# Layer 0's expert block: scalings and sums in parts between transfers, and a 512-column fill after each transfer in place of a wait for an expert tile

## What is computed

```python
h = _layernorm(x) * (1 + cb) + sb                      # per batch element: scale, then shift
logits = einsum('bnc,ec->bne', h, router_w);  w, idx = top_k(softmax(logits), 2);  w /= w.sum(-1)
hid = gelu(einsum('bnc,efc->bnef', h, w1) + b1)        # 512 hidden columns
out_all = einsum('bnef,ecf->bnec', hid, w2) + b2
x = x + gb * sum_k(out_all[idx_k] * w_k)               # only the two chosen experts are computed
h = _layernorm(x) * (1 + ca1) + sa1                    # layer 1 begins
```

## Time and profile before

| what | value |
|---|---|
| median of three executions | 1414.41 us (1411.29 to 1415.12) |
| the profiled execution, its own time | 1412.28 us |
| its span in the trace | 1410.6 us |
| PE, DVE, ACT, POOL busy over the span | 90%, 73%, 65%, 36% |
| `experts0`, from the first load of rows to the next stage's first matmul | 185.88 to 403.18 us |
| in that stretch, mean granted clock of TensorE | 0.94 |

### The profile page before, as it was taken

The page is one execution under the profiler, slowest core; times in us unless marked ns, Lnnn a source line. Parts: engine busy times, 40 slices in busy tenths (PEclk is TensorE's granted clock), DMA queues, the critical chain, the costliest instruction groups (busy, mean ns, idle before and its releaser), DMA issues. The chain is left out here.

```text
span 1410.6 us, 28627 instructions
## 1 busy us (share of the span) xinstructions
PE 1275.9 (90%) x9145; PEld 817.9 (58%) x9146; DVE 1030.0 (73%) x2720; ACT 918.1 (65%) x1320; POOL 511.8 (36%) x608
## 2 busy tenths in 40 slices
PE   6999768989886778999999999998999989998999
PEld 3877668988863423333334433333434357778898
DVE  5656266667568669888888878888988857787554
ACT  4565523333355487888888878888888848774232
POOL 5337835466449242222201222220122200388800
PEclk9999779999988799999999999999999989999999
DMA  8980112332316722222222222222022014011211
GB/s 258 222 53 24 36 58 87 97 80 72 85 53 232 201 46 37 43 41 39 32 34 33 41 39 41 42 35 38 24 42 37 9 48 139 17 57 57 71 35 32
DMA packets 112673, 93.96 MB, mean 67 GB/s; under 512 B 20034, under 2 KB 98336, under 8 KB 112544
## 3 DMA queue, kind: packets, MB, share of 16 engines
q1 hardware_dynamic: 101192, 76.18, 25.0%
q0 software_dynamic: 6144, 12.73, 3.1%
q10 hardware_dynamic: 5208, 3.43, 1.0%
HBM read 50.40 MB, written 41.89 MB: 65 GB/s over the span
## 5 line engine op out<-in xcount | busy, mean ns | idle before, releaser
L2446 ACT ACTIVATE probs<-scores_ps 128x1024 f32<-128x1024 f32 x512 | 507.2, 1027 | 86.2 <-PE scores_ps L2473 81.5
L2473 PE MATMUL scores_ps<-q_pack,k_pack 64*128 64x512 f32 x1024 | 246.6, 494 | 36.1 <-ACT probs L2446 21.2
L2490 PE MATMUL pv_ps<-probs,v_pad 128*32 128x512 f32 x2048 | 275.9, 611 | 0.0
L2473 PEld LDWEIGHTS scores_ps<-q_pack,k_pack 64*128 64x128 f32 x1024 | 96.2, 185 | 309.6 <-issue 153.5
L2366 POOL TENSOR_TENSOR squares<-sparse_scores 128x512 f32<-128x512 f32 x32 | 41.0, 1280 | 474.2 <-DVE sparse_scores L2611 474.1
L1406 ACT ACTIVATE hidden_experts<-pre_experts 128x512 f32<-128x512 f32 x94 | 59.3, 631 | 130.2 <-DVE pre_experts L1340 66.5
L2683 DVE TENSOR_SCALAR_CACHE_REDUCE junk<-sparse_scores,at 128x1024 f32<-128x1024 f32 x96 | 122.8, 1279 | 3.4
L1428 PE MATMUL up_ps_experts<-x_t_experts,up_weights_now_experts 128*128 128x128 f32 x752 | 108.2, 289 | 16.4 <-issue 7.7
L1428 PEld LDWEIGHTS up_ps_experts<-x_t_experts,up_weights_now_experts 128*128 128x128 f32 x752 | 96.1, 200 | 22.6 <-DVE up_weights_now_experts L1335 11.1
L1435 PE MATMUL down_ps_experts<-weights_t,hidden_experts 128*128 x736 | 100.5, 281 | 0.2 <-issue 0.2
L1435 PEld LDWEIGHTS down_ps_experts<-weights_t,hidden_experts 128*128 128x128 f32 x736 | 92.7, 198 | 0.0
(11 more groups left out here) (416 smaller groups left out, 2493.0 us busy)
## 6 DMA issues: line engine op xcount, KB each, us to landing
q_pack<-q_pieces_dram SPq DMA_DIRECT2D x120, 64.0 KB
k_pack<-k_pieces_dram SPq DMA_DIRECT2D x120, 64.0 KB
expert_rows_dram<-zeros SPq DMA_DIRECT2D x1, 6400.0 KB, 23.0
x_rows_experts<-expert_rows_dram SPq DMA_DIRECT2D x25, 256.0 KB
expert_rows_dram<-y_rows_experts SPq DMA_DIRECT2D x46, 128.0 KB
q_pieces_dram<-q_pieces_prep SPq DMA_DIRECT2D x8, 512.0 KB, 3.6
k_pieces_dram<-k_pieces_prep SPq DMA_DIRECT2D x8, 512.0 KB, 4.1
expert_rows_dram<-zeros SPq DMA_DIRECT2D x1, 2640.0 KB, 40.0
```

The costliest lines, as they stand in the source:

```text
L2446: act.activation(probs[:, kt % 2, 2 * pair : 2 * pair + 2, c * 512 : c * 512 + 512], scores_ps[n % 2][:].rearrange("p (h t) -> p h t", h=2 ...
L2473: ins = pe.matmul(scores_ps[n % 2][:, head * 512 : head * 512 + 512], k_pack[group % 2][rows, pair, kt * P : kt * P + P].bitcast(F32R), q_ ...
L2490: ins = pe.matmul(pv_ps[32 * j : 32 * j + 32, c, :], v_pad[:, group % 2, kt, j, :], probs[:, kt % 2, j, c * 512 : c * 512 + 512], start=(k ...
```

## The change

The block in `front` and `experts0` is changed in four ways.

1. The scaling and shifting of b = 2 goes into `front`, behind its last send, as eight POOL instructions of 256 columns (`hq.2.0` to `hq.2.7`: four that multiply, then four that add). That of b = 3 is cut likewise, and one of its eight parts stands behind each of the first eight sends of b = 2.
2. The waits for tiles (`next_tile`) are gone. Behind each send and fetch in `experts0` POOL fills a tile that nothing reads (`unread`, 128 x 512), and waits for that fill.
3. The sums of b = 0 and 1 are cut in two halves, ten instructions of 512 columns each. Those of b = 0 stand behind fetches 1 to 10 of b = 1, in place of the fills. Of b = 1's, eight run in one go when its rows have landed, and two behind the first two fetches of b = 2. The fetches of b = 1 get a semaphore of their own.
4. DVE takes the statistics of b = 0 at step 16 in place of 13; both inversions on POOL stand behind the last fetch.

```diff
+QUARTERS = 4
+    def scale_and_shift_part(self, pool, step, b, i):
+        at = b * NT + i % QUARTERS * (NT // QUARTERS)
+        h = self.h[:, at : at + NT // QUARTERS, :]
+        if i == QUARTERS:
+            step.settle()
+        op, by = ((ALU.mult, CB), (ALU.add, SB))[i // QUARTERS]
+        step(pool.tensor_tensor(h, h, bc(self.mod0[:, b, MOD0_PARTS.index(by), :], NT // QUARTERS), op))
...
-sd.1.12 sd.1.13 sd.1.14 sd.1.15 wk.10 ce2.3.1 no2.3.1 tu2.3.1 h2t.3.1 lg.3.1 lgk.3.1 be.1 po.1 exps gates ix.1 te.1
+sd.1.12 sd.1.13 sd.1.14 sd.1.15 hq.2.0 hq.2.1 hq.2.2 hq.2.3 hq.2.4 hq.2.5 hq.2.6 hq.2.7 wk.10 ce2.3.1 no2.3.1 tu2.3.1 h2t.3.1 lg.3.1 lgk.3.1 be.1 po.1 exps gates ix.1 te.1
...
-    STATS_AT = (13, 20)
+    STATS_AT = (16, 20)
+    ADDED_FIRST = 8
...
-                tile_at = [0]
-                def next_tile():
-                    tile_at[0] += 1
-                    pool.wait_ge(y_ready, tile_at[0] + 2)
+                fills = [0]
+                def fill():
+                    fills[0] += 1
+                    pool.memset(unread[:], 0.0).then_inc(filled, 1)
+                    pool.wait_ge(filled, fills[0])
                 for b in range(B):
                     if b >= SENT_EARLY:
-                        moe.scale_and_shift(pool, step, b)
                         step.settle()
-                        moe.send_rows(g, pool, b, apart=next_tile)
+                        for i in range(SEND_PARTS):
+                            moe.send_rows(g, pool, b, i, SEND_PARTS, apart=fill)
+                            if b + 1 < B and i < 2 * QUARTERS:
+                                moe.scale_and_shift_part(pool, step, b + 1, i)
                     pool.wait_ge(g.rows_sent[b], 16 * 2 * NT)
                     pool.sem_inc(rows_here, moe.tiles)
                 pool.sem_inc(rows_here, max(moe.tiles, 2 * UNROLL))
-                for b in range(B - 1):
-                    pool.wait_ge(y_free, b * (2 * AHEAD) + (2 * AHEAD + 1))
-                    tile_at[0] = max(tile_at[0], (b + 1) * moe.tiles)
-                    gather(pool, g, picked, b, [(k, n) for k in range(2) for n in range(NT)], g.rows_picked, apart=next_tile)
-                    if 1 <= b <= EARLY:
-                        pool.wait_ge(var_ready, b)
-                        g.ln1.invert(pool, b - 1).then_inc(rstd_ready, 1)
-                    pool.wait_ge(g.rows_picked, (b + 1) * (16 * 2 * NT))
-                    if b < EARLY:
-                        for part in weighted_sum(g, picked, b, NT):
-                            part(pool, step)
+                sums = [weighted_sum(g, picked, b, NT // 2) for b in range(EARLY)]
+                def add_up(b):
+                    sums[b].pop(0)(pool, step)
+                    if not sums[b]:
                         pool.sem_inc(summed, 1)
+                def fetch(b, sem, of, behind):
+                    for i, (n, k) in enumerate([(n, k) for k in range(2) for n in range(NT)]):
+                        gather(pool, g, picked, b, [(k, n)], sem)
+                        if i not in behind:
+                            fill()
+                        else:
+                            if of == 0 and i == behind[0]:
+                                pool.wait_ge(g.rows_picked, 16 * 2 * NT)
+                            add_up(of)
+                pool.wait_ge(y_free, 2 * AHEAD + 1)
+                fetch(0, g.rows_picked, None, ())
+                pool.wait_ge(y_free, 2 * (2 * AHEAD) + 1)
+                fetch(1, g.second_picked, 0, range(1, 11))
+                pool.wait_ge(g.second_picked, 16 * 2 * NT)
+                for _ in range(ADDED_FIRST):
+                    add_up(1)
+                pool.wait_ge(y_free, 3 * (2 * AHEAD) + 1)
+                fetch(2, g.rows_picked, 1, range(10 - ADDED_FIRST))
+                for b in range(EARLY):
+                    pool.wait_ge(var_ready, b + 1)
+                    g.ln1.invert(pool, b).then_inc(rstd_ready, 1)
+                pool.wait_ge(g.rows_picked, 2 * (16 * 2 * NT))
                 pool.wait_ge(rstd_ready, EARLY)
```

More of the change, by code:

```diff
@@ L615, in scale_and_shift, with scale_and_shift_part @@
                     moe.scale_and_shift(pool, step, b)
+                def scale_and_shift_part(b, i):
+                    if i == 0:
+                        for h in range(2):
+                            wait_made(pool, "tu2", b, h)
+                    moe.scale_and_shift_part(pool, step, b, i)
                 def send(b, q):
@@ L635, in _ @@
                         h2=scale_and_shift,
+                        hq=scale_and_shift_part,
                         sd=send,
@@ L1231, in experts0 @@
         y_rows = a.sb("y_rows", [P, UNROLL, C])
+        unread = a.sb("unread", [P, 512])
+        filled = a.sem("filled")
         xt_ps = a.ps("xt_ps", [C, UNROLL, P])
@@ L1482, in __init__ @@
         self.rows_picked = a.sem("rows_picked")
+        self.second_picked = a.sem("second_rows_picked")
         self.zeros = a.sb("zeros", [P, C])
```

## The result

| | before | changed |
|---|---|---|
| median | 1412.95 us (4 executions, 1411.29 to 1415.12) | 1400.85 us (4, 1399.54 to 1403.22) |
| ratio | | 0.9921, 95% interval 0.9901 to 0.9941 |
| profiled execution, own time and span | 1412.28, 1410.6 us | 1399.65, 1397.9 us |

The change makes the kernel 12.1 us faster. Forecast were 1392 us and 1386 to 1404. The record doesn't say on which chip these executions ran; it does for every experiment.

What follows compares the result with a forecast made beforehand. PE was taken to bound the expert block at 7.71 us a step, with 28.0 us lost to late signals and copies held by POOL arithmetic. Terms -21.4 - 1.1 - 2.7 + 0.9 + 3.2 = -21.1 gave 1392 us, range 1386 to 1404.

Steps and rivals of the forecast that it cites:

- The late signals: Expert block, second, third, fifth, seventh stretch: signals late behind transfers 1.26 us apart; fills spacing them 1.80 win back 21.4 us.
- The first rival: Late signals in the expert block don't come from transfer spacing: 1413 us, no change, chance 0.07; milder form 1400, chance 0.13.
- Fills: Some 70 POOL fills of 0.54 us in the expert block hold copies under the free 0.64 us: cost nothing.
- scaling of b = 3 in parts: Expert block: POOL parts of 0.75 us delay copies of weights by about what is free: -1.1 us.
- the third rival: Expert block: fills hold up DVE's copies and make DVE the bound: 1421 us, chance 0.05.
- The sums in halves: Expert block: 1.2 us parts meet copies half the time at random places, costing 1.8 us, not 4.5: -2.7.
- Statistics at step 16: Expert block: statistics of b = 0 move from under late signals to a stretch without them: +0.9 us.
- The front: Eight scaling parts of b = 2 in front hold up DVE's last router chain, seven instructions delayed: +3.2 us.
- fourth rival: Expert block: POOL is late and DVE waits for the first sum some 3 us: 1395 us, chance 0.04.

Runs made afterwards that it cites:

- e6: Kernel before with a next_tile that does not wait, all 80 transfers in runs at 1.26 us; chip 0: 1480.72 us, ratio 1.0476 to the kernel before.
- e7: Changed kernel without its fills, all else kept, on chip 12: 1459.84 us, ratio 1.0335 to the kernel before.
- e8: Kernel before with one edit, a fill in place of each next_tile wait, on chip 12: 1397.24 us, ratio 0.9897 to the kernel before.
- e1: Changed kernel without its fills, all else kept, on chip 2: 1395.93 us, ratio 1.0026 to the kernel before.
- e9: Changed kernel with each half sum cut into two instructions of 256 columns, same places; chip 4: 1394.59 us, ratio 1.0020 to the kernel before.
- e3: Changed kernel with both sums wide (1024 columns), ahead of the next fetches; chip 2: 1397.76 us, ratio 1.0036 to the kernel before.
- e5: Changed kernel with both sums wide and the scaling of b = 2 at the expert block's start; chip 0: 1399.27 us, ratio 0.9898 to the kernel before.
- e10: Changed kernel with sums in 256-column parts and the scaling of b = 2 at the expert block's start; chip 4: 1396.54 us, ratio 1.0031 to the kernel before.
- e0_after_again: Changed kernel, unchanged, run again on chip 0: 1397.08 us, ratio 0.9893 to the kernel before.

## Why the forecast held, and where it was off

**The late signals, forecast -21.4.** The mechanism is right for the kind of chip on which the first two traces were taken, and the spacing is shown to be the cause there. Without any pacing the kernel before is 67.5 us slower on chip 0 (e6); without its fills the changed kernel is 48.3 us slower than the kernel before on chip 12 (e7); and a fill behind each transfer, alone, gains 14.3 (e8). From the second, third, fifth and seventh stretch 6.3, -0.3, 4.7 and 5.9 us came back, 16.7 in all; the sums and statistics that also lie in them have the rest (below). On chips 2 and 4 the kernel before takes 20.6 to 20.8 us less than in the result; but chips may differ otherwise too, since fills alone take 1397.24 on chip 12 and 1393.51 on chip 2. From these I estimate that late signals cost it 17 to 21 us. The first rival, no gain from spacing, is refuted on chips 0 and 12. On chips 2 and 4 its outcome holds, though not for its reason: e1 shows no late signal to be avoided. There the change itself wasn't run, but its variants are 0.2 to 0.4% slower than the kernel before. That the forecast held is thus in part luck: I took the late signals for a property of the kernel, and on a chip like 2 or 4 the same change would have brought nothing. The Trainium skill's rule that DMA doesn't contend with a compute engine ("SBUF — State Buffer", "Who interferes with whom") is one on the ports of SBUF, and chip 12 doesn't contradict it. DVE's instructions behind the standstill take 0.69, 0.28 and 0.42 us there, as elsewhere; it is the signals that are late. What fails is what I drew from the rule, that spacing could then do nothing for PE: DVE and ACT did 0.00 us of work in 5.1 us beside sends.

**Fills, forecast 0; scaling of b = 3 in parts, -1.1.** To mark 13 the loss was to be nothing and is 1.0 us. Fills do hold copies a little: the median copy takes 0.472 us in place of 0.417, and 0.418 in e1, which has no fills. But without fills (e1) the loss to mark 12 is 0.7 where it is 1.0 and 1.2 with them, so the third rival (fills make DVE the bound) doesn't hold.

**The sums in halves, forecast -2.7 (from 4.5 to 1.8): the step that failed.** I said that a copy between fetches "finds POOL in arithmetic about half the time" and "at a random place". It finds it nine times in ten and near its start (the two copies above are 0.13 and 0.05 us ahead of it). In the fourth and fifth stretch the loss is 4.1 us where 0.9 was due to the sum: 3.2 more. e9 shows that parts of 256 columns take it away. Whether halves between fetches are any better than one wide sum stays open for the first sum (4.4 against 2.0 in e3 and 4.2 in e5); for the second they are, since a wide one meets the statistics.

**Statistics at step 16, forecast +0.9, and the second sum.** In the sixth to last stretch 4.5 us are lost where 2.7 was forecast (0.9 for the sum, 0.9 for each statistics): 1.8 more. Of this 1.2 is in the last stretch, which holds the statistics of b = 1 in both kernels: 0.93 before, 2.14 now, with 18 POOL instructions in it where there were 5. I took the price of the statistics from a place without transfers. The traces narrow down what raises it. It isn't the two inversions (POOL L1734, 3.29 us for the pair, at 376.14): in e9 and e10 none lies in the last stretch, and the loss is 2.21 and 2.15. It goes with the transfers there. The profiles with 7 to 10 fetches and about as many fills lose 1.88 to 2.21; e1, with 6 fetches and no fills, 1.50; those with none to 4 fetches and no fills 0.85 to 1.01. What share fetches and fills have isn't separated. e9 says that it isn't the length of the sum's parts.

**The front, forecast +3.2:** 2.25. The mechanism was right; four instructions were held for the 0.40 to 0.47 us worked out, not seven, and four more for 0.08 to 0.16. One of the four has a single input, which the forecast didn't count among those that can be held.

**The sum.** -21.1 + 3.2 (first sum) + 1.8 (behind it) + 1.0 (to mark 13) - 0.95 (front) gives -16.05; the marks say -16.46, of which 0.26 is a shorter step from mark 0 to 1 and the rest the rounding of terms. The result's median has -12.1, the same two kernels on chip 0 have 1413.19 - 1397.08 = -16.1. POOL was in time at both sums, as worked out (fourth rival).

**A better version.** The fills alone, put where `next_tile` stood, do what the whole change does: 0.9897 on chip 12 where the change has 0.9893 on chip 0, and 1.0017 on chip 2. None of the six kernels run on chips 2 and 4 beats the kernel before there. Fills with quarter sums, without the scaling in front, is e10; on a chip with late signals it wasn't run.

## What to carry to other kernels

Keep indirect transfers of POOL apart beside a loop of other engines: 1.8 us was enough on all four chips, 1.26 us wasn't on two, and nothing between was tried. A fill that nothing reads is a pacer that doesn't depend on how far the loop has come, where a wait for a count is over at once when the loop is ahead. If POOL must do arithmetic between transfers beside DVE copies, cut it until one piece holds a copy for less than the copy may be late; pieces needn't meet copies at random but can fall into step with them. Keep wide pieces away from other DVE work of the loop, such as the statistics here. Compare two kernels on one chip, and ask on more than one chip whether the gain is there.

## What the runs showed of the hardware

- One program with a transfer each 1.26 us runs in 1395.93 us on chip 2 and in 1459.84 on chip 12, and the kernel before in 1392 us on chips 2 and 4 and in 1411.5 to 1413.4 on chips 0 and 12. None of the four chips lay between. Why the chips differ, and what holds up the signals, the traces don't say. A trace of the kernel before on chip 2 or 4 wasn't taken, so that its own late signals are missing there is inferred from its time and from e1's trace.
- On chips 0 and 12, 1.8 us from transfer to transfer shows no late signal (e0_after_again, e5, e8); 1.26 stops ACT for up to 13.6 us at a run of 16 (e6).
- On chip 12, after PE had stood still for 4.54 us, the granted clock was 0.50 (1.2 of 2.4 GHz) in the stretch from 218.70 to 224.60.
- A copy of DVE that starts together with a POOL instruction on two SBUF inputs ended 0.3 us behind it at each length seen: 1.70 us beside 1.28, and 0.83 beside 0.61. A DVE instruction with one SBUF input is held too: the statistics' TENSOR_SCALAR of 8 columns took 1.66 us beside a part of 2.42 (e3) and 0.34 in the changed kernel.
